# Transposes of weighted values and of the last state as pairs of 64-row tiles over two banks, with the step orders written anew

## The chip, the cores and the metric

The kernel runs on one core of one Trainium2 chip. The metric is the device time of one execution in microseconds (us). Each kernel is timed several times, and the median is compared.

## The reference, cut to what matters

The input `x` is 64 batches of 64 rows by 256 columns, and `ctx` has the same shape. Four cross-attention layers follow one another:

```python
# layer 0: attention over the 256 columns of each batch, with 64x64 weights
Mn = Wn @ inorm(x) + bn;  Mm = Wm @ inorm(ctx) + bm
A  = softmax(Mn^T Mm);    x = Wo @ (Wl @ ctx + bl) A^T + bo + x
# layers 1 and 2: 16 heads of 16 over the 64 rows of a batch
a = layer_norm(ctx, gamma, beta)
Q = x @ Wq.T;  K = a @ Wk.T;  V = a @ Wv.T
out = softmax(Q K^T / 4) V                 # per batch and head
x = x + tanh(gate) * (out @ Wo.T)
# layer 3: one head over 256 columns, keys and values from ctx
x = x + alpha * (softmax((x @ Wq.T)(ctx @ Wk.T)^T / 16) (ctx @ Wv.T)) @ Wo.T
```

Everything is float32. The products that need the precision are made of three passes over split operands (a `_hi` part and a `_lo` part).

## The kernel before, in words

The 64 batches are worked on in 8 groups of 8. A group is 512 tokens, and the state lies in SBUF with features on the partitions and tokens along the free axis. A prologue loads and prepares the weights and does layer 0 of the first group. Each pass of the loop then does layers 1, 2 and 3 of its group, and beside them layer 0 and the layer norm of the next group. The last pass has no next group.

The order of work on TensorE (PE), ScalarE (ACT) and VectorE (DVE) is written out by hand in tables (lines 38 to 66), one for each engine, with a second set for the prologue. A word such as `T2.0-1` is a step of a layer and its indices. Each engine runs its own table in strict order, and semaphores tie the three together. The steps that are spoken of below:

- `xT`, `cT`: transposes of the next group's x and ctx (L453), copied out by ACT (L776, L780). `nT`: the normalised ctx (L468). `Mn`, `Mm`: the two products of layer 0 (L525).
- `V1`, `V2`, `V3`, `K1`, `K2`, `K3`, `Q1`, `Q2`: projections (L389 to L391). ACT copies V out at L807, K at L795, Q at L818.
- `S1`, `S2`: scores of layers 1 and 2 in eight strips (L656). DVE takes the maximum (L1055) and writes the shifted scores (L1059), of which there are two buffers. ACT takes the exponential (`X`, L856).
- `T1`, `T2`: transposes of the probabilities (L677) and ACT's copies (L870). `A1`, `A2`: probabilities times values (L731). DVE normalises them into `attn` (L1098, L1100).
- `AT1`, `AT2`: transposes of half a group's `attn` (L544). ACT copies the result to `attnT_hi` (L822), then DVE writes the rest as `attnT_lo` (L1022).
- `O1`, `O2`: output projections of both parts (L389 to L391). DVE adds them to the state (L1031). `H` and `L` split the state (ACT L837, DVE L990) for the next `Q`.
- `S0`, `X0`, `T0`, `A0`: layer 0 of the next group (L641, L851, L677/L872, L724).
- `S3`, `X3`, `T3`, `PV`: layer 3. `XN`: the state after layer 2, transposed back to tokens by features (L552, ACT copy L826), to which DVE adds `PV` (L1043).

Every step that fills PSUM takes the next of the 8 banks in the order of PE's table (`fills_of`, L108). So a fill waits until the eighth fill before it has been read. A step may take one or two banks; `turn_halves` (L671) transposes each 128-row block as two 64-row halves, the upper into one bank and the lower into another.

Of the kernel before, what the change touches and what calls it, by code (L numbers as in the profile page):

```python
# [21 lines left out]
P = 128  # L22
# [37 lines left out]
    cT.0 xT.0-1 cT.1 Wq1.0 Wk1.0 NM.1 NM.0 TG.0 Wo1.0 Wq2.0 Wv1.0 Wk2.0 Mn.0-1 Mm.0-1 Wo3T.0 nT.0-1 KB.1 VW3.0 X0.0-2 M3.0  # L60
    X0.3 T0.0-1 X0.4 T0.2-3 X0.5 Wv2.0 X0.6-7 T0.4 VB1.0 T0.5 Wo2.0 KB.2 T0.6-7 H.0 K1.0 VB2.0 OB.1 Q1.0 K1.1 H.1 OB.2
# [1289 lines left out]
```

## Time and profile before

| | us |
|---|---|
| median of 3 runs | 617.71 (616.09 to 618.76) |
| the profiled execution | 619.04 |
| its span, first to last instruction | 616.9 |
| PE busy | 570.0 |
| DVE busy | 469.0 |
| ACT busy | 469.4 |
| POOL busy | 118.0 |

The busy times are sums over the whole span. The loop repeats every 70.3 us, so a steady pass is best read as four stretches, named here by the steps at their ends. All examples are from the pass that begins at 269.5 us. Matmuls overlap one another, so what a step costs PE is the time from its first instruction to that of the next step, and not the sum of the durations.

### The profile page before, as it was taken

Reading aid. Unit: us, or ns where it says so; the run is one execution under the profiler, and the core shown is the slowest. Engines: PE = TensorE matmul, PEld = TensorE weight load, DVE = VectorE, ACT = ScalarE, POOL = GpSimd, SP = SyncE. Lnnn points to the kernel's source line nnn. Section 1 sums busy time; section 2 is a strip of 40 time slices with the busy share of each in tenths; the row PEclk is TensorE's granted clock in tenths of the full one; section 3 lists DMA queues with packets and bytes.
Section 4 is the critical chain, followed back from the end, with each engine's and each line's share of the span. In section 5 each row is a group of like instructions: output and inputs, shape, how many; then the busy total and the mean of one; then the engine's idle time right before and its main releaser. Section 6 shows DMA issues by size and latency. Waiting matters only on the chain.

```text
span 616.9 us, 25805 instructions
## 1 busy us (share of the span) xinstructions
PE 570.0 (92%) x10867; PEld 502.2 (81%) x10867; DVE 469.0 (76%) x1023; ACT 469.4 (76%) x961; POOL 118.0 (19%) x132
## 2 busy tenths in 40 slices
PE   1799999999999999999999999999999999999885
PEld 1678788888888887988889887998889888998774
DVE  5785879676986879687786869778796869876553
ACT  0799878878787779867788869867788768868651
POOL 3503070103310070102500060101601051000000
PEclk9899999999999999999999999999999999999978
DMA  6420001110020100210020100210020100010001
GB/s 154 161 75 2 2 3 44 35 37 1 3 75 4 34 2 4 74 36 2 2 75 3 36 2 3 74 36 3 2 75 2 37 2 2 3 36 3 3 2 34
DMA packets 18499, 18.32 MB, mean 30 GB/s; under 512 B 1828, under 2 KB 18340, under 8 KB 18404
## 3 DMA queue, kind: packets, MB, share of 16 engines
q1 hardware_dynamic: 18024, 16.55, 8.5%
q8 instruction: 87, 1.43, 1.0%
q0 software_dynamic: 320, 0.26, 0.4%
q14 instruction: 8, 0.07, 0.0%
q10 hardware_dynamic: 60, 0.01, 0.0%
HBM read 12.63 MB, written 4.19 MB: 27 GB/s over the span
## 4 chain that ended last, share of the span: by engine, by line
PE 65%; DVE 15%; ACT 10%; issue 6%; DMA 1%; SPq 1%; POOL 0%; DVEq 0%; ACTq 0%; POOLq 0%
PE psum L389 10%; PE psum L731 8%; PE psum L677 8%; PE psum L391 8%; PE psum L390 8%; DVE negmax L1055 7%; PE psum L724 5%; DVE shifted L1059 4%; PE psum L641 4%; ACT work L856 3%; PE psum L656 3%; PE psum L544 3%; ACT v L807 2%; PE psum L453 2%; DMA mrow_u<-in_mask_dram 1%
## 5 line engine op out<-in xcount | busy, mean ns | idle before, releaser
L1059 DVE TENSOR_TENSOR shifted<-psum,negmax 128x512 f32<-128x512 f32 x128 | 88.5, 692 | 10.5 <-ACT work L856 5.6
L856 ACT ACTIVATE work<-shifted 128x512 f32<-128x512 f32 x128 | 79.1, 631 | 18.8 <-DVE shifted L1059 17.8
L870 ACT ACTIVATE work<-psum,group_mask 128x512 f32<-128x512 f32 x128 | 80.4, 696 | 16.4 <-PE psum L677 16.4
L1055 DVE TENSOR_REDUCE negmax<-psum 128x8 f32<-128x512 f32 x128 | 87.3, 682 | 5.9 <-PE psum L656 5.3
L677 PEld LDWEIGHTS psum<-const,work 64*128 64x128 f32 x1536 | 55.8, 141 | 33.4 <-issue 32.0
L677 PE MATMUL psum<-const,work 64*128 64x64 f32 x1536 | 65.0, 229 | 18.7 <-ACT work L856 16.6
L731 PEld LDWEIGHTS psum<-v,work 128*64 128x64 f32 x2048 | 63.9, 141 | 8.1 <-issue 5.9
L731 PE MATMUL psum<-v,work 128*64 128x34 f32 x2048 | 67.5, 227 | 0.0
L851 ACT ACTIVATE work<-psum,negmax 128x256 f32<-128x256 f32 x128 | 50.2, 511 | 12.2 <-DVE negmax L1051 12.2
L807 ACT ACTIVATE v<-psum 64x256 f32<-64x256 f32 x128 | 49.7, 388 | 10.0 <-PE psum L391 8.7
L795 ACT ACTIVATE kbd<-psum,own_bias,const 128x512 f32<-128x512 f32 x64 | 46.2, 777 | 4.8 <-PE psum L391 4.4
L1051 DVE TENSOR_REDUCE negmax<-psum 128x2 f32<-128x512 f32 x64 | 40.5, 682 | 9.2 <-PE psum L641 9.2
L1244 POOL TENSOR_SCALAR var_eps<-mean_var 128x8 f32<-128x8 f32 x8 | 2.0, 248 | 221.4 <-DVE mean_var L1116 221.4
L1022 DVE TENSOR_TENSOR attnT_lo<-psum,attnT_hi 128x512 fp32r<-128x512 f32 x32 | 22.1, 689 | 26.0 <-ACT attnT_hi L822 26.0
L389 PE MATMUL psum<-attnT_hi,wT_o_hi 128*128 128x256 f32 x128 | 39.4, 308 | 1.7 <-DVE attnT_lo L1022 0.3
L656 PE MATMUL psum<-kbd,work 32*64 32x128 f32 x2048 | 39.3, 283 | 1.2 <-ACT kbd L795 0.9
L389 PE MATMUL psum<-wT_v_hi,nT_hi 128*128 128x256 f32 x128 | 39.3, 307 | 0.0
L872 ACT ACTIVATE work<-psum 128x512 f32<-128x512 f32 x64 | 35.6, 616 | 4.6 <-PE psum L677 4.6
L724 PE MATMUL psum<-v,work 128*64 128x65 f32 x1024 | 36.7, 223 | 0.5 <-issue 0.5
L390 PE MATMUL psum<-attnT_lo,wT_o_hi 128*128 128x256 f32 x128 | 36.7, 287 | 0.0
L391 PE MATMUL psum<-attnT_hi,wT_o_lo 128*128 128x256 f32 x128 | 36.6, 286 | 0.0
L389 PE MATMUL psum<-state_hi,wT_q_hi 128*128 128x256 f32 x128 | 36.5, 285 | 0.0
(181 smaller groups left out, 1536.1 us busy)
## 6 DMA issues: line engine op xcount, KB each, us to landing
x_raw<-in_x_dram SPq DMA_DIRECT2D x8, 512.0 KB, 4.3
c_raw<-in_ctx_dram SPq DMA_DIRECT2D x8, 512.0 KB, 5.0
...
```

The source lines that it names most:

```text
L389: pe.matmul(o, lh, rh, start=first, stop=False)
L390: pe.matmul(o, lh, rl, start=False, stop=False)
L391: return pe.matmul(o, ll, rh, start=False, stop=last)
L656: mm_ = pe.matmul(to[C * c:C * c + C, P * n:P * n + P], queries[rows, k, C * b:C * b + C], kbd[l - 1][rows, k, b].rearrange("p q s -> p (q ...
L677: mm_ = pe.transpose(banks[h][:, C * n:C * n + C], src[rows], ident[rows, rows])
L724: mm_ = pe.matmul(o[C * q:C * q + C, cols], probsT[:, at + q, t0:t0 + C], v0[:, batch_of(i), s, :], start=s == 0, stop=s == 1)
L731: mm_ = pe.matmul(o[C * c:C * c + C, 2 * VW * j:2 * VW * (j + 1)], probsT[:, at + c, C * j:C * j + C], v2[l - 1][:, 2 * i + c, j].rearrang ...
L807: ins = act.activation(values[C * q:C * q + C, c, q, :, :, 0:HD], o[C * c:C * c + C, :].rearrange("k (p j q v) -> k q p j v", p=2, q=2, v= ...
L856: act.activation(probs[:, exp_row(g, l, i, last), :], shifted[:, i % 2, :], ACT.Exp).then_inc(exps, 1)
L870: act.activation(probsT[:, at, :], o[:], ACT.Copy, scale=group_mask[:, 2 * i + c:2 * i + c + 1]).then_inc(free, 1)
L1055: dve.tensor_reduce(negmax[:, i % 2, :], sv, AX_X, ALU.max, negate=True).then_inc(rowmax, 1)
L1059: dve.tensor_tensor(shifted[:, i % 2, :].rearrange("t (j k) -> t j k", k=C), sv, negmax[:, i % 2, :].unsqueeze(2).broadcast_to([P, NJ, C]) ...
```

## The change

`AT` was four transposes of 128 by 128 into one bank. It is now `turn_halves`: eight transposes of 64 rows by 128 columns, four into each of two banks. ACT and DVE copy each bank by itself, half the tokens of every pair at a time, so each has two instructions of 128x256 where it had one of 128x512. `XN` was two steps of four transposes; it is now one step of sixteen over two banks, and still two copies of 128x512 on ACT.

```diff
@@ fills_of
-            if kind == "P" or kind == "S" or kind == "A" and (l or i % 2 == 0):
+            if kind == "P" and l in ("AT1", "AT2"):
+                fills += [step + (c,) for c in range(2)]
+            elif kind == "P" or kind == "S" or kind == "A" and (l or i % 2 == 0):
@@ TensorE, proj_step
                 elif name in ("AT1", "AT2"):
-                    for q in range(2):
-                        for k in range(NK):
-                            mm_ = pe.transpose(o[:, (2 * q + k) * P:(2 * q + k + 1) * P],
-                                               attn[:, 2 * i + q, NJ * k:NJ * k + NJ, :].rearrange("t n d -> t (n d)"), ident)
+                    o2, signal2 = start_fill(g, step, last, 1)
+                    turn_halves((o, o2), (signal, signal2), [attn[:, 2 * i + q, NJ * k:NJ * k + NJ, :].rearrange("t n d -> t (n d)")
+                                                             for q in range(2) for k in range(NK)])
+                    return
...
                 elif name == "XN":
-                    for q in range(2):
-                        p = 2 * i + q
-                        for k in range(NK):
-                            mm_ = pe.transpose(o[:, D * q + P * k:D * q + P * k + P], state[:, k, P * p:P * p + P], ident)
+                    o2, signal2 = start_fill(g, ("P", "XN", 1), last)
+                    turn_halves((o, o2), (signal, signal2), [state[:, k, P * p:P * p + P] for p in range(NP) for k in range(NK)])
+                    return
@@ ScalarE, proj_step
                 elif name in ("AT1", "AT2"):
-                    o, _ = filled(g, step, last)
-                    act.activation(attnT[0][:].rearrange("f k (p t) -> f p k t", p=2),
-                                   o[:].rearrange("f (p k t) -> f p k t", p=2, k=NK), ACT.Copy).then_inc(attn_hi, 1)
+                    for h in range(2):
+                        o, _ = filled(g, step, last, h)
+                        act.activation(attnT[0][:].rearrange("f k (p h t) -> f h p k t", p=2, h=2)[:, h],
+                                       o[:, 0:4 * C].rearrange("f (p k t) -> f p k t", p=2, k=NK), ACT.Copy).then_inc(attn_hi, 1)
@@ VectorE, proj_step
                 elif name in ("AT1", "AT2"):
...
+                    for h in range(2):
+                        o, free, _ = filled(g, step, last, h)
+                        dve.wait_ge(attn_hi, 8 * g + (4 * int(name[2]) - 3 + 2 * i + h))
+                        hi, lo = [t[:].rearrange("f k (p h t) -> f h p k t", p=2, h=2)[:, h] for t in attnT]
+                        dve.tensor_tensor(lo, o[:, 0:4 * C].rearrange("f (p k t) -> f p k t", p=2, k=NK), hi.bitcast(F32),
+                                          ALU.subtract).then_inc(free, 1)
```

All six tables are written anew. A line of PE's, for example:

```diff
-    V1.0 S1.0-3 V2.0 Q1.1 V3.0 S1.4-7 T1.0-1 V1.1 K3.0 A1.0-1 T1.2-3 xT.0-1 AT1.0 K2.0 O1.0 A1.2-3 K2.1 AT1.1 Q2.0 O1.1
+    V1.0 S1.0-3 Q1.1 V2.0 V3.0 S1.4-7 T1.0-1 K3.0 V1.1 A1.0-1 T1.2-3 AT1.0 K2.0 O1.0 A1.2-3 K2.1 AT1.1 Q2.0 O1.1 S2.0-3
```

Three places matter. The first is on PE in the middle of layer 1, from `A1.0-1` to the start of `K2.0`. Before:

```order
L731 MATMUL psum<-v_1,work 64x34 x32
L677 MATMUL psum<-const,work 128x64 x32
L453 MATMUL psum<-const,x_raw 128x64 x16
L544 MATMUL psum<-const,attn 128x128 x4
L389 MATMUL psum<-nT_hi,wT_k_hi 128x512
L390 MATMUL psum<-nT_lo,wT_k_hi 128x512
```

And after (line numbers are those of the changed kernel, L678 is `turn_halves`):

```order
L732 MATMUL psum<-v_1,work 64x34 x32
L678 MATMUL psum<-const,work 128x64 x32
L678 MATMUL psum<-const,attn 128x64 x8
L391 MATMUL psum<-nT_hi,wT_k_hi 128x512
L392 MATMUL psum<-nT_lo,wT_k_hi 128x512
```

The transposes of x (`xT`) have left this place, and the four transposes of `attn` are eight of half the columns.

The second place is on ACT around the first strips of layer 2's scores. `state_hi` is `H.3`, `shifted` the exponentials `X2`, `v_2` is `V2.1`, `scratch` is `V3.1`, and the `work<-psum` of 128x2x256 is `Q2.1`. Before:

```order
L837 ACTIVATE state_hi<-state 128x512
L856 ACTIVATE work<-shifted 128x512
L807 ACTIVATE v_2<-psum 64x2x8x16 x4
L856 ACTIVATE work<-shifted 128x512
L769 REGISTER_ALU
L815 ACTIVATE scratch<-psum 128x512
L818 ACTIVATE work<-psum 128x2x256
L856 ACTIVATE work<-shifted 128x512 x2
L789 ACTIVATE mn_hi<-psum,scale_col 128x512 x2
```

And after:

```order
L840 ACTIVATE state_hi<-state 128x512
L770 REGISTER_ALU
L777 ACTIVATE xT<-psum 128x8x64
L859 ACTIVATE work<-shifted 128x512
L858 REGISTER_ALU
L859 ACTIVATE work<-shifted 128x512
L770 REGISTER_ALU
L808 ACTIVATE v_2<-psum 64x2x8x16 x4
L777 ACTIVATE xT<-psum 128x8x64
L816 ACTIVATE scratch<-psum 128x512
L858 REGISTER_ALU
L859 ACTIVATE work<-shifted 128x512
```

Both copies of `xT` now stand here, and the second exponential comes ahead of `V2.1`. On DVE the split of the state, `L.3`, has moved in the same place from behind the first strip to behind the second.

The third place is on PE towards the end of a pass, from `S3.1` on. Before:

```order
L667 MATMUL psum<-scratch,state 64x64 x8
L724 MATMUL psum<-v,work 64x65 x24
L552 MATMUL psum<-const,state 128x128 x4
L701 MATMUL psum<-const,probs 128x128
L389 MATMUL psum<-nT_hi,wT_k_hi 128x512
```

And after:

```order
L668 MATMUL psum<-scratch,state 64x64 x8
L678 MATMUL psum<-const,work 128x64 x16
L678 MATMUL psum<-const,state 128x64 x16
L702 MATMUL psum<-const,probs 128x128
L391 MATMUL psum<-state_hi,wT_q_hi 128x256
```

`XN` is one step ahead of `T3.0`, `Q1.0` comes before `K1.1`, and the last of layer 0's `A0` steps (L724) now follow `T3.1`, directly ahead of `PV`. On ACT the copies of `T3.1`, `XN`, `Q1.0` and `K1.1` and the split `H.1` follow one another in that order at the end of the pass, and on DVE `L.1` stands behind `PV`.

## Rows read from the trace of the kernel before

**Rows 1.** The page's part 4: chain that ended last, share of the span by engine.
```profile
PE 65%; DVE 15%; ACT 10%; issue 6%; DMA 1%; SPq 1%; POOL 0%; DVEq 0%; ACTq 0%; POOLq 0%
```

**Rows 2.** Busy time by window: start:end, length, PE, PEld, DVE, ACT, POOL, clock.
```profile
277.30:297.40 20.10, 19.85 (x346) 17.54 (x346) 13.86 (x38) 14.76 (x28) 8.07 (x8) 1.00 0.01 2
297.40:311.75 14.35, 13.66 (x305) 11.50 (x299) 13.94 (x22) 12.37 (x24) 3.50 (x3) 1.00 0.01 2
311.75:339.80 28.05, 27.93 (x542) 25.18 (x542) 21.28 (x52) 22.60 (x49) 2.76 (x5) 1.00 0.14 43
269.50:277.30 7.80, 6.80 (x165) 6.21 (x164) 7.29 (x13) 6.38 (x14) 0.00 (x0) 1.00 0.21 69
```

**Rows 3.** Timeline, 284.6 to 287.6: start us, duration us, engine, line, tiles, count.
```profile
284.71 0.72 PE L453 MATMUL psum<-const,x_raw 64*128 64x64 f32 x16
...
285.36 0.66 PE L544 MATMUL psum<-const,attn 128*128 128x128 f32 x4
...
285.77 0.48 PE L389 MATMUL psum<-nT_hi,wT_k_hi 128*128 128x512 f32 x1
...
286.06 0.60 ACT L822 ACTIVATE attnT_hi<-psum 128x512 fp32r<-128x512 f32 x1 [1.49 <-PE psum L544]
...
286.69 0.69 DVE L1022 TENSOR_TENSOR attnT_lo<-psum,attnT_hi 128x512 fp32r<-128x512 f32 x1 [0.71 <-ACT attnT_hi L822]
...
287.52 0.35 PE L389 MATMUL psum<-attnT_hi,wT_o_hi 128*128 128x256 f32 x1
```

**Rows 4.** Timeline of PE, 322 to 329: `T0.0-3`, then `XN.0` and `O2.1`.
```profile
322.58 1.22 PE L677 MATMUL psum<-const,work 64*128 64x64 f32 x32
323.60 0.36 PE L641 MATMUL psum<-mm_hi,mn_hi 64*128 64x256 f32 x2
...
328.44 0.66 PE L552 MATMUL psum<-const,state 128*128 128x128 f32 x4
328.85 0.36 PE L389 MATMUL psum<-attnT_hi,wT_o_hi 128*128 128x256 f32 x1
```

**Rows 5.** Lines, shapes apart: count, busy us, mean ns of one, idle before.
```profile
L1100 DVE TENSOR_TENSOR attn<-psum,recip 128x256 f32<-128x256 f32 x64 | 27.2, 424 | 2.2
...
L544 PE MATMUL psum<-const,attn 128*128 128x128 f32 x128 | 20.9, 288 | 0.0
...
L776 ACT ACTIVATE xT<-psum 128x512 f32<-128x512 f32 x16 | 8.6, 586 | 0.3 <-PE psum L453 0.3
```

**Rows 6.** Timeline of ACT in the prologue: a copy of 128x256 from PSUM.
```profile
53.15 0.40 ACT L883 ACTIVATE scratch<-psum 128x256 f32<-128x256 f32 x1
```

**Rows 7.** Timeline, 297 to 312: `H.3`, `X2.0`, `V2.1`, `Mn`, `S2.4`, `cT`.
```profile
297.31 0.63 ACT L837 ACTIVATE state_hi<-state 128x512 fp32r<-128x512 f32 x1 [1.66 <-DVE state L1031]
...
298.89 0.63 ACT L856 ACTIVATE work<-shifted 128x512 f32<-128x512 f32 x1 [0.94 <-DVE shifted L1059]
...
299.43 1.57 ACT L807 ACTIVATE v<-psum 64x256 f32<-64x256 f32 x4
...
304.12 1.25 ACT L789 ACTIVATE mn_hi<-psum,scale_col 128x512 fp32r<-128x512 f32 x2
...
304.82 1.41 DVE L1016 SCALAR_TENSOR_TENSOR mn_lo<-psum,scale_col,mn_hi 128x512 fp32r<-128x512 f32 x2
...
306.24 0.69 DVE L1055 TENSOR_REDUCE negmax<-psum 128x8 f32<-128x512 f32 x1
...
311.77 0.43 PE L453 MATMUL psum<-const,c_raw 64*128 64x64 f32 x7
```

**Rows 8.** Timeline, end of a pass: `H.1` on ACT, the next pass's `S1.0-3`.
```profile
337.96 0.62 ACT L837 ACTIVATE state_hi<-state_in 128x512 fp32r<-128x512 f32 x1
...
339.81 1.21 PE L656 MATMUL psum<-kbd,work 32*64 32x128 f32 x64
```

**Rows 9.** Busy time by window, the end of the prologue and the first steps.
```profile
45.00:77.00 32.00, 29.20 (x488) 25.49 (x488) 22.27 (x55) 28.70 (x69) 5.69 (x7) 1.00 0.01 2
```

**Rows 10.** Busy time by window in the last pass; the clock is third from last.
```profile
595.00:605.00 10.00, 9.84 (x112) 8.88 (x110) 2.93 (x7) 3.43 (x6) 0.00 (x0) 0.50 0.01 2
```

More of the change, by code:

```diff
@@ L38 @@
 PE_ORDER = """
-    V1.0 S1.0-3 V2.0 Q1.1 V3.0 S1.4-7 T1.0-1 V1.1 K3.0 A1.0-1 T1.2-3 xT.0-1 AT1.0 K2.0 O1.0 A1.2-3 K2.1 AT1.1 Q2.0 O1.1
-    S2.0-3 V2.1 V3.1 Q2.1 V0.0-1 Mn.0-1 T2.0 S2.4-7 T2.1 K3.1 Mm.0-1 A2.0-1 cT.0-1 T2.2 nT.0-1 AT2.0 T2.3 S0.0-3 A2.2-3
-    O2.0 AT2.1 K1.0 T0.0-3 S0.4-7 A0.0-1 S3.0 A0.2-3 T0.4-5 XN.0 O2.1 T3.0 T0.6-7 A0.4 S3.1 A0.5-7 XN.1 T3.1 K1.1 Q1.0
+    V1.0 S1.0-3 Q1.1 V2.0 V3.0 S1.4-7 T1.0-1 K3.0 V1.1 A1.0-1 T1.2-3 AT1.0 K2.0 O1.0 A1.2-3 K2.1 AT1.1 Q2.0 O1.1 S2.0-3
+    xT.0-1 V2.1 V3.1 Q2.1 V0.0-1 Mn.0-1 T2.0 S2.4-7 T2.1 Mm.0-1 K3.1 A2.0-1 cT.0-1 T2.2 nT.0-1 T2.3 A2.2 AT2.0 S0.0-3 A2.3
+    O2.0 T0.0-1 AT2.1 K1.0 T0.2-3 S0.4-7 A0.0-2 S3.0 A0.3 T0.4-5 O2.1 A0.4-5 S3.1 T0.6-7 XN.0-1 T3.0 Q1.0 K1.1 T3.1 A0.6-7
     PV.0-1
@@ L44 @@
 ACT_ORDER = """
-    SC.0 V1.0 X1.0 V2.0 Q1.1 X1.1-2 V3.0 X1.3 T1.0 X1.4-5 T1.1 X1.6 K3.0 X1.7 V1.1 AT1.0 T1.2-3 H.2 xT.0-1 K2.0 AT1.1 K2.1
-    Q2.0 H.3 X2.0 V2.1 X2.1 V3.1 Q2.1 X2.2-3 Mn.0-1 T2.0-1 X2.4 K3.1 X2.5 Mm.0 X2.6 Mm.1 X2.7 cT.0-1 T2.2 nT.0-1 AT2.0
-    T2.3 X0.0-3 AT2.1 K1.0 T0.0-3 X0.4-7 T0.4 X3.0 H.0 T0.5-7 XN.0 T3.0 X3.1 T3.1 XN.1 K1.1 Q1.0 H.1
+    SC.0 V1.0 Q1.1 X1.0-1 V2.0 X1.2 V3.0 X1.3 T1.0 X1.4 T1.1 X1.5 K3.0 X1.6-7 V1.1 AT1.0 T1.2-3 H.2 K2.0 AT1.1 K2.1 Q2.0
+    H.3 xT.0 X2.0-1 V2.1 xT.1 V3.1 X2.2 Q2.1 X2.3 Mn.0-1 T2.0-1 Mm.0 X2.4-5 K3.1 Mm.1 X2.6-7 cT.0-1 T2.2 nT.0-1 T2.3 AT2.0
@@ L48 @@
+    X0.0-3 AT2.1 T0.0-1 K1.0 T0.2-3 X0.4-6 T0.4-5 X0.7 X3.0 H.0 X3.1 T0.6 T3.0 T0.7 T3.1 XN.0-1 Q1.0 K1.1 H.1
 """
 DVE_ORDER = """
-    S1.0-7 A1.0 ST.0 A1.1 ST.1-2 AT1.0 ST.3 MV.0 O1.0 A1.2-3 L.2 AT1.1 O1.1 S2.0 L.3 S2.1-3 V0.0-1 Mn.0-1 S2.4-7 Mm.0-1
-    A2.0-1 cT.0-1 nT.0-1 AT2.0 S0.0-1 A2.2-3 S0.2-3 O2.0 AT2.1 S0.4-7 S3.0 A0.1 A0.3 O2.1 S3.1 A0.5 X3.0 L.0 X3.1 A0.7 L.1
-    PV.0-1
+    S1.0-7 ST.0 A1.0-1 ST.1 AT1.0 ST.2-3 O1.0 MV.0 A1.2 L.2 A1.3 AT1.1 O1.1 S2.0-1 L.3 S2.2-3 V0.0-1 Mn.0-1 S2.4-7 Mm.0-1
@@ L53 @@
+    A2.0-1 cT.0-1 nT.0-1 A2.2 S0.0 AT2.0 S0.1-2 A2.3 S0.3 O2.0 AT2.1 S0.4-6 A0.1 S3.0 S0.7 A0.3 O2.1 L.0 A0.5 X3.0 S3.1
+    X3.1 A0.7 PV.0-1 L.1
 """
 PE_FIRST = """
-    MT.0 W0T.0 GT.0 MS.0 cT.0-1 xT.0-1 W0.0 Wq1.0 Wk1.0 Wo1.0 Wq2.0 V0.0-1 Wv1.0 Wk2.0 Mn.0-1 Mm.0-1 Wo3T.0 nT.0-1 VW3.0
-    S0.0-3 M3.0 T0.0-1 S0.4-5 T0.2-3 S0.6-7 A0.0 Wv2.0 A0.1-3 T0.4-5 Wo2.0 VB1.0 T0.6-7 A0.4 K1.0 A0.5 K1.1 VB2.0 A0.6-7
-    Q1.0
+    MT.0 MS.0 GT.0 xT.0-1 cT.0-1 Wq1.0 W0T.0 Wk1.0 Wv1.0 nT.0-1 Mn.0-1 Mm.0-1 W0.0 Wo3T.0 S0.0-3 V0.0-1 Wq2.0 M3.0 Wk2.0
@@ L58 @@
+    VB1.0 T0.0-3 S0.4-5 Wo1.0 VW3.0 S0.6-7 A0.0-1 T0.4-5 Wv2.0 A0.2 K1.0 A0.3 T0.6-7 VB2.0 Wo2.0 A0.4-5 K1.1 A0.6-7 Q1.0
 """
 ACT_FIRST = """
[L60 to L61 removed]
+    xT.0-1 cT.0-1 Wq1.0 NM.1 NM.0 Wk1.0 Wv1.0 Mn.0-1 Mm.0 nT.0-1 Mm.1 Wo3T.0 KB.1 X0.0 TG.0 X0.1 Wq2.0 X0.2-3 M3.0 Wk2.0
@@ L62 @@
+    T0.0 VB1.0 T0.1-3 X0.4 Wo1.0 X0.5 VW3.0 KB.2 X0.6-7 T0.4 Wv2.0 T0.5 Wo2.0 T0.6-7 H.0 K1.0 OB.1 VB2.0 K1.1 Q1.0 H.1
+    OB.2
 """
 DVE_FIRST = """
-    MT.0 WB.0 ON.0 MS.0 ST.0 W0T.0 GT.0 ST.1-2 TG.0 ST.3 MV.0 NB.0 Wq1.0 cT.0-1 W0.0 Wk1.0 Wo1.0 Wq2.0 Wv1.0 V0.0-1 Wk2.0
-    Mn.0-1 Mm.0-1 nT.0 S0.0 nT.1 S0.1-2 VW3.0 S0.3 M3.0 S0.4-7 Wv2.0 A0.1 A0.3 Wo2.0 L.0 A0.5 A0.7 L.1
+    MT.0 MS.0 GT.0 WB.0 TG.0 ST.0-3 MV.0 cT.0 NB.0 W0T.0 cT.1 Wq1.0 ON.0 Wk1.0 Mn.0 Wv1.0 Mn.1 nT.0-1 Mm.0-1 W0.0 S0.0-3
@@ L66 @@
+    V0.0-1 Wq2.0 M3.0 Wk2.0 S0.4-6 Wo1.0 VW3.0 A0.1 S0.7 Wv2.0 A0.3 Wo2.0 L.0 A0.5 A0.7 L.1
 """
@@ L488, in proj_step @@
                     return
-                if name == "PV" and i:
+                if name in ("PV", "XN") and i:
                     return
-                used = {"O1": [("P", "AT1", i)], "O2": [("P", "AT2", i)], "PV": [("T", 3, 0), ("T", 3, 1)]}.get(name, [])
+                used = {"O1": [("P", "AT1", i, h) for h in range(2)], "O2": [("P", "AT2", i, h) for h in range(2)], "PV": [("T", 3, 0), ("T", 3, 1)]}.get(name, [])
                 if name in ("AT1", "AT2"):
@@ L820, in proj_step @@
                 elif name in ("AT1", "AT2"):
-                    o, _ = filled(g, step, last)
-                    act.activation(attnT[0][:].rearrange("f k (p t) -> f p k t", p=2),
-                                   o[:].rearrange("f (p k t) -> f p k t", p=2, k=NK), ACT.Copy).then_inc(attn_hi, 1)
+                    for h in range(2):
+                        o, _ = filled(g, step, last, h)
+                        act.activation(attnT[0][:].rearrange("f k (p h t) -> f h p k t", p=2, h=2)[:, h],
+                                       o[:, 0:4 * C].rearrange("f (p k t) -> f p k t", p=2, k=NK), ACT.Copy).then_inc(attn_hi, 1)
                 elif name == "XN":
                     o, free = filled(g, step, last)
-                    act.activation(result[:, 2 * i:2 * i + 2, :], o[:].rearrange("s (q h) -> s q h", q=2), ACT.Copy).then_inc(free, 1)
+                    act.activation(result[:].rearrange("t p (k h f) -> t h p k f", k=NK, h=2)[:, i],
+                                   o[:].rearrange("t (p k f) -> t p k f", p=NP, k=NK), ACT.Copy).then_inc(free, 1)
             def state_high(g, n, last):
@@ L979, in _, with filled @@
         def _(dve):
-            def filled(g, step, last):
-                bk, n = fill(g, step, last)
+            def filled(g, step, last, c=0):
+                bk, n = fill(g, step, last, c)
                 dve.wait_ge(full[bk], n)
```

6 lines of the change are left out of this document (removed).

## The prediction

> **What bounds the kernel now.** I read the chain of waits first, then the busy time by window over one steady pass, then the timeline inside each window. The chain is PE for 65% of the span, DVE for 15% and ACT for 10% [rows 1], so neither "PE is the bound" nor its opposite holds everywhere. The windows show where each is true [rows 2]. A pass takes 70.3 us and falls into four stretches:
>
> - A, from `T1.0` to `S2.0-3`, 20.1 us: PE busy 19.85. PE sets the pace.
> - B, from the first strips of `S2` to `cT`, 14.35 us: DVE busy 13.94, PE 13.66. DVE sets the pace with ACT close beside it.
> - C, from `cT` to the next pass's `S1.0-3`, 28.05 us: PE busy 27.93. PE sets the pace.
> - D, from `S1.0-3` to `T1.0`, 7.8 us: PE busy 6.80. `T1.0` waits for the exponentials of four strips, that is for DVE and ACT.
>
> So PE time removed in A and C is worth itself. The same time removed in B or D is worth nothing, and work added there to ACT or DVE costs.
>
> **The transposes on PE.** Four transposes of 128x128 hold PE from 285.36 to 285.77, 0.41 us [rows 3]. The new form is not unknown: `turn_halves` is already used for the probabilities, where 32 pieces of 64 columns take 1.02 us, 32 ns each [rows 4]. Eight pieces are 0.26 us, so an `AT` saves 0.15 us. The mean duration of one transpose, 288 ns, is latency and doesn't enter [rows 5]. `XN` before is two steps of about 0.41 [rows 4]; sixteen pieces are 0.51; saved 0.31.
>
> **The chain behind AT.** In A, `AT1` is followed by one projection and then by `O1`, which needs both parts of the result. From the transposes to `O1` it takes 2.16 us: 0.70 to ACT's start, 0.63 to DVE's start, 0.83 to `O1` [rows 3]. PE's own work in between is 0.41 plus about 1.48 for six matmuls of 512 columns, so some 0.27 is stall, twice a pass. After the change: 0.70 less 0.15 is 0.55; ACT's first copy of 128x256 takes 0.40 [rows 6] and DVE starts 0.43 after it; DVE's two of 0.424 each [rows 5] run while ACT's second is done, 0.85; then the same 0.14 to PE. Together 1.97, saved 0.2 for each of `AT1.0` and `AT1.1`. The bounds are 0 (ACT or DVE is late with other work) and 0.4 (the whole stall and the 0.15 go). `AT2.0` and `AT2.1` in C have other steps behind them and give the 0.15 each.
>
> Two copies instead of one make ACT longer by 2 x 0.40 - 0.60 = 0.2 and DVE by 2 x 0.42 - 0.69 = 0.16 per `AT`, 0.8 and 0.64 us per pass. In A and C they are covered: ACT is busy 14.76 of 20.10 and 22.60 of 28.05 [rows 2]. The register instructions that the table adds on ACT are bounded by the same cover.
>
> **The move of xT.** It leaves A, where its sixteen transposes hold PE from 284.71 to 285.36, 0.65 us [rows 3]: all of it gained. `AT1.0` comes nearer to `A1.1`, but `T1.2-3` still stands between. SP's loads wait for `nT`, which isn't moved against its neighbours, and none is near.
>
> It goes to B, where PE has 0.7 us of slack but ACT has two more copies of 0.586 [rows 5]. `xT.0` fits into the 0.94 us in which ACT waits for the first shifted strip [rows 7]. The second doesn't, and here the new order matters more: `X2.1` now stands ahead of `V2.1`. The second strip comes one DVE pace (0.68 + 0.69 less overlap, 1.32 us) after the first, so not before 298.89 + 1.32 = 300.21. Before, ACT began `V2.1` at 299.43 and reached `Mn` at 304.12, 4.7 us later, with about 0.35 idle [rows 7]. Now it has the same instructions, less that idle, plus `xT.1` at about 0.5: 300.21 + 4.85 = 305.05, late by 0.9. DVE's `Mn` (304.82) needs ACT's, and the strips `S2.4-7` (306.24) come behind it, then `cT` at 311.77 [rows 7]. I take +0.8 for B. Bounds: 0 if DVE has slack that I don't see, +1.2 if both copies count in full.
>
> **The rest of the orders.** In C, saved 2 x 0.15 + 0.31 = 0.6. `T0.2-3` is held apart from `T0.0-1` and `A0.2` comes early, which may cost a few tenths behind ACT. In D, `Q1.1` goes ahead of `X1.0` on ACT; ACT's sum is unchanged, but it must wait for PE's `Q1.1`: +0.2 (0 to 0.5). At the end of the pass `L.1` stands behind `PV` on DVE and `H.1` behind four copies on ACT. Before, `H.1` ended at 338.58, 1.2 us ahead of `S1.0-3` at 339.81 [rows 8]. I charge nothing in the sum, and a rival below has the rest.
>
> **The sum.** Per pass: A -0.65 - 2 x 0.2 = -1.05; B +0.8; C -0.6; D +0.2; together -0.65 us. Seven passes have a next group: -4.6. The last has no `xT` and no front, so A gives -0.4 and C -0.6, part of it at the lower clock: for 595 to 605 the granted clock is 0.50, which is 1.2 GHz [rows 10], and every PE price there doubles, +0.2 more. Last pass -1.2. The prologue's statistics and first products come earlier, but ACT must do the same work before `S1.0-3` and is already busy 28.70 of 32.00 at its end [rows 9]: 0, bounds -1.5 and +1.5. In all -5.8 us on the profiled execution's 619.04 (span 616.9 and 2.1 around it), 613.2. That execution is 1.3 above the median of the runs shown, so against the median 617.71 - 5.8 = 611.9, rounded to 612.
>
> **The rivals.**
>
> 1. B costs nothing and the whole chain gain in A comes. For it: ACT idles 2 us of B's 14.35. Against: `Mn` sits right behind the dense part. Then each pass gives 0.65 + 0.8 + A's 0.55 + C's 0.6 less D's 0.2, less what I doubt, about 1.5 us: 7 x 1.5 + 1.2 = 12, 606.
>
> 2. The gain is given back and nothing is left. PE's 1.65 us per pass in A and C meet +1.2 in B, +0.5 in D: 7 x 0 to 1, some 1.2 from the last pass: 616.5. For it: ACT and DVE each get some 0.7 us more per pass, and B and D, 22 of 70 us, are theirs. A page speaks for this side: the Trainium skill, "TensorEngine Tiling (Array Packing)", section "PSUM Bottleneck", says that tiling speeds up TensorE but not the copies out of PSUM, which may then be the bottleneck. By that rule alone the sum would stand at this rival's figure. The trace agrees for B and D and disagrees for A and C.
>
> 3. Slower: the end of the pass becomes a queue. ACT gets to `K1.1` only after `T3.1`, two copies of `XN` at some 0.5 and `Q1.0` at 0.5; PE behind `T3.1` has `A0.6-7`, `PV` and `V1.0`, about 3.6 us, before `S1.0-3` needs `K1.1`. ACT needs 0.3 + 1.0 + 0.5 + 1.45 = 3.3, then `H.1` 0.6, and DVE's `L.1` 0.7 and the first strip behind it. It decides from 0.4 us of lateness of `T3.1`'s partner copies on. If `S1` strips start 1.3 us late, D grows by that, and with B at +1.2 a pass loses 0.9: 7 x 0.9 - 1.2 = +5, 623. Against it: the `A0` and `K1.1` steps give ACT slack earlier.
>
> 4. The change doesn't do what it says: the row pairs of `attn` run one behind another. Then 8 pieces cost no less than 4, A and C lose 0.9 per pass against the forecast: 618. Against it: the same form runs at 32 ns a piece now [rows 4], from the same kind of source.
>
> **How the numbers follow.** The forecast has 0.43, with its own range 609 to 614.5; rival 1 has 0.21, rival 2 0.20, rival 3 0.12, rival 4 0.04. A difference under 0.5%, 3.1 us, can't be told from no change. Faster by more: the forecast and rival 1, 0.64, and a share of rival 2, 0.03: 0.67. Same: the rest of rival 2, rival 4 and a bit of 3: 0.22. Slower: 0.11. The range 605.5 to 619 holds rival 1 and 2 and leaves out rival 3 and the far end of rival 1.
>
> **What would show it.** Right: the steady pass falls from 70.3 to about 69.6; from `AT1.0` to `O1.0` it takes about 1.95 us; eight pieces of `attn` hold PE 0.26; ACT starts `Mn` some 7.6 us after `H.3` and not 6.8; B is longer than 14.35 by 0.6 to 1; C is shorter by about 0.6. Wrong: B unchanged (rival 1), D above 8.5 with `S1.0-3` waiting for ACT's K copy (rival 3), or 64-column pieces of `attn` over 50 ns apart (rival 4). A lower clock in a steady pass would upset all of it; there it is 1.00 now [rows 2].

## The result, and the profile after

The changed kernel is slower: 625.73 us, median of 6 runs, beside 618.5 for the kernel before; ratio 1.0124, 95% interval 1.0106 to 1.0142. The forecast was 612, in a range of 605.5 to 619, with 0.11 for slower. It was wrong in size and in sign.

The profiled span went from 616.9 to 624.4 us. The chain is still PE's, more than before [rows 1]:

```profile
PE 69%; ACT 13%; DVE 8%; issue 7%; DMA 2%; SPq 1%; DVEq 0%; ACTq 0%
```

The same four stretches, in the order A, B, C, D of [rows 2] (columns as there):

```profile
281.60:299.53 17.93, 17.78 (x274) 15.91 (x275) 12.49 (x38) 13.83 (x27) 4.95 (x5) 1.00 0.01 2
299.53:315.77 16.24, 15.68 (x379) 13.25 (x379) 14.96 (x24) 13.45 (x26) 7.15 (x6) 1.00 0.01 3
315.77:344.35 28.58, 27.91 (x559) 24.77 (x559) 22.31 (x56) 22.79 (x52) 2.77 (x5) 1.00 0.15 41
273.58:281.60 8.02, 6.74 (x164) 6.20 (x164) 6.90 (x12) 6.10 (x14) 0.00 (x0) 1.00 0.22 69
```

These windows end at the first strips of `S2` (299.53). [rows 2] put that edge at 297.40, which is a little inside `S2`; with the edge at the first strip in both kernels (296.30 before) and D's end at `T1.0` (277.34, 281.64), a pass compares so, in us:

| stretch | before | after | change | forecast |
|---|---|---|---|---|
| D | 7.80 | 8.06 | +0.26 | +0.2 |
| A | 18.96 | 17.89 | -1.07 | -1.05 |
| B | 15.47 | 16.24 | +0.77 | +0.8 |
| C | 28.04 | 28.58 | +0.54 | -0.6 |
| pass | 70.27 | 70.77 | +0.50 | -0.65 |

Three terms of four came as priced. C has the wrong sign. Two more things lie outside the table: the first `S1.0-3` starts at 60.99 instead of 57.19 us (the prologue, forecast 0), and the last pass takes 66.45 instead of 66.53 (forecast -1.2). The seven passes together take 496.96 instead of 493.18, 3.78 more. With 3.80 for the prologue and -0.08 for the last pass, that is the whole 7.5 us of the span.

The chain behind `AT1.0` in A, as in [rows 3], is 1.89 us from the pieces to `O1.0` (forecast 1.97; before 2.16):

```profile
289.14 0.46 PE L678 MATMUL psum<-const,attn 64*128 64x64 f32 x8
...
289.61 0.66 ACT L824 ACTIVATE attnT_hi<-psum 128x256 fp32r<-128x256 f32 x2 [0.71 <-PE psum L678]
...
290.02 0.76 DVE L1027 TENSOR_TENSOR attnT_lo<-psum,attnT_hi 128x256 fp32r<-128x256 f32 x2 [0.70 <-ACT attnT_hi L824]
...
291.03 0.28 PE L391 MATMUL psum<-attnT_hi,wT_o_hi 128*128 128x256 f32 x1
```

The eight pieces hold PE 0.39 here, not 0.26. What the four `AT` steps cost, from the first transpose to the next step's first instruction, is this:

| step | before | after |
|---|---|---|
| `AT1.0` | 0.41 | 0.39 |
| `AT1.1` | 0.36 | 0.40 |
| `AT2.0` | 0.58 | 0.28 |
| `AT2.1` | 0.35 | 0.35 |

Here are the lines of `AT2.1`, before and then after, each with the first instruction of `K1.0` behind it:

```profile
320.66 0.60 PE L544 MATMUL psum<-const,attn 128*128 128x128 f32 x4
321.01 0.48 PE L389 MATMUL psum<-nT_hi,wT_k_hi 128*128 128x512 f32 x1
```

```profile
325.14 0.41 PE L678 MATMUL psum<-const,attn 64*128 64x64 f32 x8
325.49 0.50 PE L391 MATMUL psum<-nT_hi,wT_k_hi 128*128 128x512 f32 x1
```

A piece is still 32 ns behind the last. But where PE changes between 64-row pieces and full-array matmuls, about 0.1 us is added: sixteen pieces of `T0` hold PE 0.64 ahead of a full-array step (331.69 to 332.33) and 0.55 ahead of other pieces (335.65 to 336.20). `AT2.0` now stands between two tiled steps and gains; the others have a full-array step behind them. `XN` is 0.59 (336.20 to 336.79), where its two steps were 0.41 and 0.50.

At the end of the pass, to be compared with [rows 8], the three engines do this:

```profile
341.03 1.09 PE L559 MATMUL psum<-scratch 64*64 64x256 f32 x16
...
341.66 1.47 ACT L796 ACTIVATE kbd<-psum,own_bias,const 128x512 f32<-128x512 f32 x2
...
342.44 1.66 DVE L1046 SCALAR_TENSOR_TENSOR attn<-psum,recip,attn 128x256 f32<-128x256 f32 x4 [0.18 <-issue]
...
344.35 0.62 PE L657 MATMUL psum<-kbd,work 32*64 32x128 f32 x25 [0.60 <-DVE attn L1046]
```

`V1.0` begins at 342.05 and, with the 1.62 us that it took before, would be through at 343.67. `S1.0-3` starts 0.68 later, when DVE has read `PV`. The waits (line, releaser, total us, times, longest) say that it is so in every pass:

```profile
PE psum L657 <- DVE attn L1046: 4.3, 7, 0.6
PE psum L678 <- issue: 0.8, 2, 0.6
```

The reason is in the bank numbers, which follow the order of fills and begin again at 0 in every pass. Before, PE's order has 104 fills, thirteen rounds of 8. Four `AT` with two banks make 108, so at the pass boundary the fills of banks 0 to 3 no longer look back 8 fills but 4: `PV.0` and `PV.1` take banks 2 and 3, and `S1.1` and `S1.2`, four fills later, take the same ones. (The fills of banks 4 to 7 look back 12.)

In the prologue (windows of before, then of after), `nT` and the next steps stand earlier and PE runs into two waits. The first is 2.99 us ahead of `nT` at 23.84. The profile names no releaser, but ACT's last copy of the normalised ctx ends at 23.63. The second is 2.81 us ahead of `S0.0-3` at 33.72, for DVE. Behind each, PE's pieces take about double, and from 32 to 40 us the granted clock is near its lower level. The kernel before has one such place, 2.32 us idle ahead of 23.79 and a clock of 0.63 behind it:

```profile
24.00:28.00 4.00, 3.62 (x75) 3.29 (x74) 2.04 (x7) 3.97 (x10) 2.13 (x2) 0.63 0.01 4
...
32.00:36.00 4.00, 3.60 (x59) 2.96 (x50) 3.35 (x6) 3.94 (x15) 0.00 (x0) 1.00 0.26 79
36.00:40.00 4.00, 3.62 (x44) 2.96 (x42) 3.67 (x8) 3.67 (x11) 0.00 (x0) 1.00 0.60 206
```

```profile
24.00:28.00 4.00, 3.97 (x84) 3.08 (x87) 0.99 (x3) 3.16 (x9) 1.17 (x1) 1.00 0.02 4
...
32.00:36.00 4.00, 2.28 (x21) 2.31 (x23) 2.49 (x7) 2.87 (x12) 0.00 (x0) 0.61 0.00 0
36.00:40.00 4.00, 4.00 (x77) 3.59 (x75) 3.23 (x6) 2.12 (x6) 0.00 (x0) 0.53 0.11 9
```

### The profile page after: what moved, and what is told of

Its sections match the earlier page's. It is cut to its first block, busy times and chain, and to the rows that moved or that the text cites. A ratio compares the mean times of both kernels' runs of the same rounds, so it can differ in the third digit from the quotient of the medians.

```text
span 624.4 us, 26526 instructions
## 1 busy us (share of the span) xinstructions
PE 571.1 (91%) x11059; PEld 501.8 (80%) x11059; DVE 471.5 (76%) x1055; ACT 469.9 (75%) x993; POOL 121.9 (20%) x132
## 4 chain that ended last, share of the span: by engine, by line
PE 69%; ACT 13%; DVE 8%; issue 7%; DMA 2%; SPq 1%; DVEq 0%; ACTq 0%
PE psum L678 12%; PE psum L391 10%; PE psum L732 10%; PE psum L393 8%; PE psum L392 8%; PE psum L725 5%; ACT work L859 4%; PE psum L657 4%; PE psum L642 4%; ACT v L808 3%; DVE negmax L1058 3%; DVE shifted L1062 2%; DVE attn L1046 2%; PE psum L470 2%; PE psum L668 1%
## 5 line engine op out<-in xcount | busy, mean ns | idle before, releaser
L678 PE MATMUL psum<-const,work 64*128 64x64 f32 x1536 | 65.4, 229 | 18.2 <-ACT work L859 17.5
L678 PEld LDWEIGHTS psum<-const,work 64*128 64x128 f32 x1536 | 55.5, 140 | 31.3 <-issue 28.6
L732 PE MATMUL psum<-v,work 128*64 128x34 f32 x2048 | 69.3, 227 | 0.9 <-ACT work L873 0.9
L854 ACT ACTIVATE work<-psum,negmax 128x256 f32<-128x256 f32 x128 | 51.9, 507 | 11.1 <-DVE negmax L1054 11.1
L1054 DVE TENSOR_REDUCE negmax<-psum 128x2 f32<-128x512 f32 x64 | 41.8, 684 | 16.6 <-PE psum L642 16.2
L391 PE MATMUL psum<-state_hi,wT_q_hi 128*128 128x256 f32 x128 | 38.6, 302 | 0.6 <-DVE state_lo L993 0.5
L657 PEld LDWEIGHTS psum<-kbd,work 32*64 32x64 f32 x2048 | 31.8, 133 | 8.7 <-issue 5.8
L1027 DVE TENSOR_TENSOR attnT_lo<-psum,attnT_hi 128x256 fp32r<-128x256 f32 x64 | 24.1, 419 | 18.9 <-ACT attnT_hi L824 18.9
L391 PE MATMUL psum<-wT_v_hi,nT_hi 128*128 128x256 f32 x128 | 37.6, 294 | 0.0
L824 ACT ACTIVATE attnT_hi<-psum 128x256 fp32r<-128x256 f32 x64 | 21.4, 395 | 21.2 <-PE psum L678 21.2
```

The source lines that it names most:

```text
L391: pe.matmul(o, lh, rh, start=first, stop=False)
L657: mm_ = pe.matmul(to[C * c:C * c + C, P * n:P * n + P], queries[rows, k, C * b:C * b + C], kbd[l - 1][rows, k, b].rearrange("p q s -> p (q ...
L678: mm_ = pe.transpose(banks[h][:, C * n:C * n + C], src[rows], ident[rows, rows])
L732: mm_ = pe.matmul(o[C * c:C * c + C, 2 * VW * j:2 * VW * (j + 1)], probsT[:, at + c, C * j:C * j + C], v2[l - 1][:, 2 * i + c, j].rearrang ...
L854: ins = act.activation(probs[:, exp_row(g, 0, i, last), D * u:D * u + D], psum[bk][:, D * u:D * u + D], ACT.Exp, bias=negmax0[:, i, u:u + 1])
```

## The experiments

Ratios are to the kernel before, timed beside each kernel. "A quiet pass" is the one that begins near 270 us; it takes 70.27 before and 70.77 after.

### The prologue's order alone

```diff
 changed kernel, with the kernel before's PE_FIRST, ACT_FIRST, DVE_FIRST
```

> The changed kernel with the three prologue tables of the kernel before; the loop is the changed one. Theory: the first S1.0-3 comes 3.8 us later in the changed kernel (60.99 against 57.19) because of the prologue's new order, so this kernel should be 3.8 us faster than the changed one, about 622, with S1.0-3 first at about 57.2. Rival: the prologue's delay comes from outside the tables (loads, memsets); then it stays at 625.7.

Measured: 1.0072 (1.0049 to 1.0095), first `S1.0-3` at 57.64, quiet pass 70.80, `S1.0-3` still waits for DVE 4.3 us. The theory held: 0.5 of the 1.24% is the prologue, about 3 us, give or take the 0.2 of each interval.

### TensorE kept busy in the prologue

```diff
-                    for k in range(NK):
+                    for _ in range(8 if name == "Wv1" else 1):   # and the loops under it, one deeper
```

> The changed kernel, with the four transposes of Wv1's first tile written eight times over into the same bank (same values), so that TensorE works in the prologue where it stood idle ahead of 23.84 us. Theory (after the idle TensorE runs at half its clock and its pieces take double, and this makes the prologue late): pieces of that stretch near 1.2 instead of 2.0 us, the first S1.0-3 1 to 3 us earlier, 622.5 to 624.5. Rival (the order, three more loads of weights ahead of T0.0, sets it): no change, 625.

Measured: 1.0126 (1.0084 to 1.0168), no gain in time. In the trace the first `S1.0-3` is at 59.84, 1.15 earlier. Two lines of PE:

```profile
24.03 1.16 PE L470 MATMUL psum<-mix,c_norm 64*64 64x64 f32 x64
...
26.93 1.07 PE L527 MATMUL psum<-c_norm,w0T 64*64 64x256 f32 x16
```

They were 1.98 and 1.96 in the changed kernel. So the doubled pieces do come from the idle time ahead of them, but what follows waits for DVE anyway (2.71 us before `S0.0-3`), the clock falls there (0.50 in 32 to 36), and most is lost again. Theory and rival each hold for a part. In another run of the same prologue (the run of moved banks, below) the clock was 1.00 from 32 us on and `S1.0-3` came at 58.29. From these single executions the order costs about 1 us, and the later fall of the clock adds up to 2.7 where it happens.

### The transposes alone, and the ring of banks

Three kernels ask what the second bank costs. The first is the kernel before with only `AT` changed; the second adds skipped banks to it so that the boundary closes; the third has no change but the skipped banks.

```diff
 kernel before; AT1 and AT2 as in the changed kernel, XN and all tables as before
```

> The kernel before with AT1 and AT2 alone as pairs of 64-row tiles over two banks; XN, all six tables as before. Theory: AT1.0 and AT1.1 to O1 fall from 2.1 to 1.9 us, AT2 gives 0.1 each, about 0.6 us less per pass, but 108 fills break the ring: S1.0-3 waits for DVE's PV, which ends at 340.87 in the pass where S1.0-3 starts at 339.81, so a pass gains about 1.1 - 0.6 = 0.5: some 618 + 3.5 = 621.5. Rival (the form is a gain wherever it stands): 614.

```diff
 the same, one bank skipped ahead of each of V1.1, K2.0, T0.4, A0.4
```

> As the run before with the ring closed by four skipped banks. Theory: 0.6 us less per pass and nothing given back, 8 passes: 618 - 5 = 613.5. Rival (ACT's and DVE's second instruction per AT cost what PE saves): 618.

```diff
 kernel before, AT as it was; one bank skipped ahead of each of K2.0, Q2.0, T2.3, K1.0
```

> The kernel before with its transposes of 128x128 in one bank as they were; only one bank of the ring is skipped behind each of the four AT steps (before K2.0, Q2.0, T2.3, K1.0), so that the fills behind find the same banks as with two-bank transposes. Theory (the second bank is the price that the two-bank transposes alone paid, 636): 632 to 637. Rival (the 64-row form itself costs, not its bank): within 1% of the kernel before, 618 to 622.

Measured: 1.0295 (1.0238 to 1.0352), 1.0612 (1.0554 to 1.0671) and 1.039 (1.0336 to 1.0444). Waits of the first and of the third:

```profile
PE psum L391 <- ACT work L873: 9.1, 7, 1.3
PE psum L658 <- DVE attn L1046: 8.9, 7, 1.4
...
PE psum L679 <- DVE cT_lo L1009: 4.0, 7, 0.6
```

```profile
PE psum L664 <- DVE attn L1051: 9.1, 7, 1.4
PE psum L397 <- ACT work L878: 8.8, 7, 1.3
...
PE psum L685 <- DVE cT_lo L1014: 3.5, 7, 0.5
```

The same three waits, though the third kernel has not one 64-row transpose more. The price is the bank, not the form: a step with two banks brings the fills behind it one nearer to the step whose bank they need. `K2.0` behind `AT1.0` then needs `T1.2`'s bank, which ACT hasn't read. I had expected the direction of the first but a fifth of its size. The second I had wrong: skipping more banks closes the boundary and shortens the distance elsewhere. The third is dearer than the 632 to 637 I gave it (641.36), and dearer than the first, so the form gives a little back; no run separates that part.

So in the old order this transpose loses 18 us, and the changed kernel loses 7. Counted by its table, `K2.0` there takes a bank of `A1.0`, because `xT`'s two fills no longer stand in between. No run takes the other orders and `XN` apart from this.

```diff
 changed kernel, one bank skipped ahead of each of K3.0, K2.0, T0.4, T0.6
```

> The changed kernel with banks skipped at four loose places, so that the 108 fills of a pass take 112 places, a whole number of rounds of 8. Theory: 108 is 4 over a multiple of 8 and each pass starts again at bank 0, so S1.1 and S1.2 of a pass get the banks of PV.0 and PV.1, filled just before, and S1.0-3 waits for DVE's PV; closing the ring takes off 0.65 us in each of 7 passes, 4.5 us: about 621, the step V1.0 to S1.0 back at 1.6 us from 2.3. Rival: S1.0-3 waits for ACT's K1.1 copy (343.13) or Q1.0 anyway, or the skipped banks make as much wait elsewhere: 625.

Measured: 1.0191 (1.0138 to 1.0243), quiet pass 70.99. The wait of `S1.0-3` for DVE is gone and others stand in its place: PE's projections now wait 4.5 us for DVE's shifted scores, 15 times. The rival was right.

### Moving only the boundary's banks

```diff
+    MOVED = {("P", "PV", 0, 0): 5, ("P", "PV", 1, 0): 4, ("S", 1, 3, 0): 6, ("P", "V2", 0, 0): 4}
+            banks.update({f: b for f, b in MOVED.items() if f in banks})
```

> The changed kernel, except that four fills at the end of a pass take other banks (PV.0 bank 5, PV.1 bank 4, S1.3 bank 6, V2.0 bank 4), so that the scores S1.0-3 need no bank that PV.0 or PV.1 used. Theory (the pass boundary's banks are the price of stretch C): the 4.3 us that TensorE waits for VectorE's attn at S1.0-3 are gone, seven times about 0.65 us: about 621. Rival (another wait takes its place, ScalarE's K1.1 or Q1.0 end as late as PV's copy): within 0.5% of the changed kernel, 625.

> As the run before, and with the prologue's three order tables of the kernel before. Theory (prologue and pass boundary are the two causes of the loss and add up): about 617 to 618, level with the kernel before. Rival (only the prologue counts): 622, as with the old prologue alone.

Measured: 1.0175 (1.0132 to 1.0218, four runs) and 1.009 (1.0062 to 1.0119), where the kernels without the moved banks had 1.0124 and 1.0072. No gain in time, and the rival of each was right. Quiet passes are 70.56 and 70.60, only 0.2 less. The trace of the first names the new wait, for `XN`'s copies:

```profile
337.80 1.08 ACT L835 ACTIVATE attn<-psum 128x512 f32<-128x512 f32 x2
...
339.03 1.09 PE L566 MATMUL psum<-scratch 64*64 64x256 f32 x16 [0.35 <-ACT attn L835]
```

ACT had stood idle 0.95 us ahead of these copies, for `T3.1`, which its order puts first.

```diff
-    ... T0.7 T3.1 XN.0-1 Q1.0 ...
+    ... T0.7 XN.0-1 T3.1 Q1.0 ...
```

> The changed kernel with the kernel before's prologue tables, the four moved banks at the end of the pass, and on ScalarE the two copies of XN ahead of T3.1's scratch copy instead of behind it (ScalarE idled 0.92 us there before T3.1 while XN lay ready, and TensorE's PV then waited 0.35 us for XN's banks). Theory (the pass boundary's wait had only moved to XN's copies): the PV wait goes, S1.0-3 starts 0.35 us earlier in each pass, ratio to the kernel before 1.004 to 1.006 against 1.009 without this edit. Rival (another wait behind it, K1.1 or the strips, takes it again): 1.009.

Measured: 1.0041 (1.0017 to 1.0065), quiet pass 70.19. `PV` starts when `A0.6-7` is through:

```profile
334.18 1.10 ACT L836 ACTIVATE attn<-psum 128x512 f32<-128x512 f32 x2
...
336.20 1.09 PE L567 MATMUL psum<-scratch 64*64 64x256 f32 x16
```

The theory held. The moved banks had given 0.2 us a pass and the copy order gives 0.4 behind them, 0.58 together. In the ratio the copy order is 0.5% (from 1.009), both together 0.3% (from the 1.0072 of the old prologue alone), with intervals of 0.2 to 0.3; seven times 0.58 would be 0.66%. The copy order without the moved banks wasn't run.

### The orders in D and B

```diff
-PE    V1.0 S1.0-3 Q1.1 V2.0 V3.0          ACT   V1.0 Q1.1 X1.0-1 V2.0 X1.2 V3.0
+PE    V1.0 S1.0-3 V2.0 Q1.1 V3.0          ACT   V1.0 X1.0 V2.0 Q1.1 X1.1-2 V3.0
```

> As the run before, and with Q1.1 behind X1.0 and V2.0 again on ScalarE and TensorE, as in the kernel before. Theory (Q1.1 ahead of X1.0 is what made stretch D 0.26 us longer): D back at 7.8 us, 7 x 0.26 = 1.8 us less, ratio 1.002. Rival (D is longer because PE's 64-row order and ST moved): D unchanged, same time.

```diff
-ACT   xT.0 X2.0-1 V2.1 xT.1 V3.1 X2.2
+ACT   xT.0 X2.0 V2.1 xT.1 X2.1 V3.1 X2.2
```

> As the run before, and on ScalarE X2.1 again behind V2.1 instead of ahead of it. Theory (X2.1 ahead of V2.1 makes ScalarE wait for the second strip and V2.1, V3.1, Mn late; that is half of stretch B's 0.77): S2.0 to S2.4 9.56 falls to 9.2, 2 to 2.5 us less, ratio 0.998 to 1.0. Rival (xT's two copies alone set B): B unchanged at 9.56.

> The best kernel so far once more, in five rounds. Theory (0.5 us less a pass than the kernel before, less two stalls of about 1 us together): ratio 0.996 to 0.998, faster by 1 to 2 us. Rival (level): 0.999 to 1.001.

Both kernels also move `Q1.1` to bank 5, where the changed kernel has it.

Measured: 1.0004 (0.9983 to 1.0025), 0.9988 (0.9959 to 1.0016), and the last again in five rounds 0.9987 (0.997 to 1.0004). Quiet passes 69.80, 69.70, 69.80. D's order was worth what I had given it and a little more (0.39 us a pass, of which D itself is 0.37). B's shows its own sign: from `S2.0` to `S2.4` it takes 9.15 instead of 9.56. But 0.29 of that is lost again ahead of `cT`, so a pass gains only 0.1. The third run met its rival, level (0.999 to 1.001), and not the 0.996 to 0.998 of its theory. The final kernel's stretches, as D, A, B, C:

```profile
267.58:275.35 7.77, 6.77 (x166) 6.25 (x166) 7.31 (x13) 6.38 (x14) 0.00 (x0) 1.00 0.21 70
275.35:293.24 17.89, 17.80 (x274) 15.89 (x275) 12.75 (x38) 13.82 (x27) 4.97 (x5) 1.00 0.01 2
293.24:309.36 16.12, 15.66 (x380) 13.24 (x379) 14.83 (x24) 13.55 (x26) 7.13 (x6) 1.00 0.01 3
309.36:337.28 27.92, 27.85 (x559) 24.75 (x559) 21.51 (x54) 22.48 (x51) 2.76 (x5) 1.00 0.15 43
```

69.70 in all, 0.57 less than before: close to the 0.65 forecast, but with other parts. C is 0.12 shorter, not 0.6. No kernel here beats the kernel before by more than the comparison can tell.

### XN alone, its place alone, and idle time that nothing explains

```diff
 kernel before; XN as in the changed kernel, at XN.1's place; ACT: T3.0 X3.1 XN.0-1 T3.1
```

> The kernel before with only XN changed: one step of sixteen 64-row transposes over its two banks, placed where XN.1 stood, and ScalarE's two copies ahead of T3.1. Attn's transposes, xT, every other place and the count of fills as in the kernel before. Theory (the form pays where it takes no more banks): XN 0.41 + 0.50 becomes 0.59, 0.3 us less a pass, 616.4 less 2.2: 614 to 615 where the kernel before has 616.4, ratio 0.9965. Rival (XN's late place brings T3.1, K1.1 and S1.0-3 late): ratio 1.002 or more.

```diff
 kernel before; XN's full transposes kept, only moved to that place
```

> The kernel before with XN's two steps of full transposes as they were, but both at the late place (XN.0 beside XN.1, and ScalarE's two copies ahead of T3.1) where the run with XN alone in row pairs had them. Theory (the added instructions of the row pairs bring stalls in which TensorE waits for nothing in the trace, not the place): ratio 0.998 to 1.002, passes of 70.3 without such stalls. Rival (the late place delays T3.1, K1.1 and S1.0-3): 1.005 to 1.008, as with the row pairs.

Measured: 1.0069 (1.0041 to 1.0097) and 1.0067 (1.0051 to 1.0083), as both rivals had it. The place costs, and the form then gives or takes nothing that can be told. My theory that the added instructions bring the loss fell. Where the second kernel loses its 4 us isn't shown: its profiled execution is its fastest (615.8), and there the quiet pass is only 0.14 longer than before. The first kernel's trace shows the step at 0.65 instead of 0.91 in a quiet pass, and in other passes this:

```profile
335.13 0.34 PE L676 MATMUL psum<-const,state 64*128 64x64 f32 x4
...
335.89 0.59 PE L676 MATMUL psum<-const,state 64*128 64x64 f32 x12 [0.42 <-issue]
```

PE stops in the middle of a step, waiting for nothing that the profile shows. The kernel before has such stops too: 0.49 us inside `A0` at 115.99, and one inside `S0` in its pass of 70.7, which only the weight loads show:

```profile
246.17 0.18 PEld L641 LDWEIGHTS psum<-mm_hi,mn_lo 64*128 64x128 f32 x1 [0.34 <-issue]
```

To see whether it hangs on where the code lies, two kernels got the same 28 extra matmuls in the prologue:

```diff
 kernel before, and the kernel of 0.9988: Wv1's four transposes eight times over
```

> The kernel before, with the four transposes of Wv1's first tile written eight times over into the same bank in the prologue, 28 matmuls more there and the same code in the passes. Theory (where blocks of instructions begin decides which passes stall): the prologue 0 to 3 us later, and some passes 0.4 to 1.1 us longer than 70.2, with idle time of TensorE that nothing in the trace explains. Rival (the kernel before has instructions to spare): every pass within 0.2 us of 70.3 and only the prologue changed.

> The best kernel so far (changed transposes, the kernel before's prologue order, moved banks, XN's copies ahead of T3.1, the old orders in D and B), with the same 28 matmuls more in the prologue. Theory (position of the code): the passes that take 70.6 us there now fall on other passes, and their sum changes by 1 us or more in either direction. Rival (the stall belongs to the late passes, whatever the code's place): passes 1 to 4 at 69.7, the last two at 69.9 and 70.6 again.

Measured: 1.0075 (1.005 to 1.01) and 1.0061 (1.0045 to 1.0077). The first `S1.0-3` is at 60.90 and 61.04, 3.7 and 3.3 us later, which is most of it: the step became 3.3 us longer at a place where PE had no idle time, and it costs its full length. Passes of the first, from the second on, are 71.02, 70.97, 70.47, 70.51, 70.21, 70.24, against 70.2 to 70.7 before. The two long ones hold a stop of 0.68 and one of 0.50, as the theory had it and against the rival's 0.2 us around 70.3:

```profile
189.84 0.92 PE L725 MATMUL psum<-v,work 128*64 128x65 f32 x24 [0.68 <-issue]
```

Of the second, two passes (70.27 and 70.82) are long. But the kernel of 0.9988 had its long passes at different places in two executions of the same code (70.60 as the seventh; then 70.28, 70.32 and 70.42 as the second, fifth and seventh). So a stop that moves from one pass to another doesn't show that the code's place moved it, and the two runs settle nothing.

The page of the first `XN` kernel has an instruction queue with 88 packets and 1.44 MB, 16 KB each, 11 in each pass, as many as a pass of the kernel before has. The Trainium skill, "Runtime: NRT & Kernel Launch", section "Instruction fetch mechanics", says that instructions come in blocks of 16 KiB and that crossing from one to the next is mostly hidden. The trace agrees on the size; whether the idle time is a late block isn't shown by any run, and stays open. Its size can't be read from the waits put down to `issue`: between 120 and 560 us they are 1.9 and 2.7 us in the two runs of the best kernel, but most of that is a gap of 0.2 to 0.4 ahead of `T2`'s pieces, which other passes have too, put down to ACT or DVE.

## Why the prediction was wrong

**The bounds of the stretches.** Right: D, A and B came within 0.06 us of their terms.

**The transposes on PE.** The 32 ns a piece was right, the price of a step wasn't. "An `AT` saves 0.15 us" left out what PE pays where it changes between pieces and full-array matmuls. The four steps save 0.02, -0.04, 0.30 and 0.00: 0.28 in all instead of 0.60. That `AT2.0` and `AT2.1` together give the 2 x 0.15 of C is luck. `XN` saves 0.32 for 0.31 because the step before took 0.91, not twice 0.41. Rival 4 had the wrong mechanism, pieces one behind another, but what it said of the cost, eight pieces no less than four, came true at three steps of four.

**The chain behind AT.** Right, 1.89 for 1.97, and 1.88 behind `AT1.1` (2.11 before). What is gained is the stall ahead of `O1`, about 0.25 each time. ACT starts 0.47 behind the first piece instead of 0.70, while PE's own pieces save next to nothing there.

**xT.** Right in both halves, -0.65 in A and +0.77 in B. In B all of it comes ahead of `S2.4` (8.80 before, 9.57 after from `S2.0` on), and ACT starts `Mn` 7.53 us after `H.3`, as forecast (7.6). Of the reason given, `X2.1` ahead of `V2.1`, the run without it leaves 0.1 in B as a whole. That the two copies more on ACT are the rest is argued; no run took them out of B.

**"In C, saved 2 x 0.15 + 0.31 = 0.6".** This step failed. The saving is there, though not as priced (`AT2.0` 0.58 to 0.28, `AT2.1` 0.35 as before, `XN` 0.91 to 0.59), but two costs that I had put at nothing stand beside it. One is `S1.0-3`'s wait for `PV`'s banks, 0.68. I had looked for lateness at the end of the pass in ACT's queue (rival 3) and not in the banks, although the diff's first lines make two fills of one; counting them, 108 against a ring of 8, would have shown it. The other is 0.5 in small steps: the new order puts a tiled step where a full-array one stood behind `O2.0` and `O2.1`, and splits `A2.2-3`. `O2.1`, which was followed by a full transpose, took 1.51 from 328.85 [rows 4]. It is now followed by tiled `A0.4-5` and takes 1.62:

```profile
331.69 0.71 PE L678 MATMUL psum<-const,work 64*128 64x64 f32 x16
332.33 0.38 PE L391 MATMUL psum<-attnT_hi,wT_o_hi 128*128 128x256 f32 x1
...
333.95 0.45 PE L725 MATMUL psum<-v,work 128*64 128x65 f32 x8
```

Of the 0.11, 0.10 lies behind the twelve matmuls: `A0.4-5` starts 0.21 after the last of them (333.74), where the transpose had started 0.11 after it. `O2.0` went from 1.54 to 1.62, `A2` and `S3.1` lost 0.12 and 0.15. This part is read from the two traces, and no run took it away; in the best kernel it is still there.

**"I charge nothing" for the prologue.** This step failed too. The cover named was ACT's busy share of 45 to 77 [rows 9]. The loss comes before it, between 20 and 42 us, in a stretch that I hadn't read: PE idles twice, 2.99 and 2.81 us, and behind each idle time its pieces take double. It is 3.8 us in the trace and 0.5% in the ratio, outside my bound of +1.5.

**D.** The term was right, +0.26 for +0.2; undoing it gave 0.39 a pass.

**The last pass.** -1.2 was wrong; it is -0.1. Which of its steps take the gain back wasn't read.

**The miss in one line.** The forecast had -5.8 us of span and +7.5 came, 13.3 apart: C 8.0 (seven times 1.14), the prologue 3.8, the last pass 1.1, and 0.4 in passes longer than the one that the table shows.

**The rivals.** Rival 1's terms don't add up to its 1.5 us a pass: 0.65 and 0.8 are 1.45, and with the other two it is more than 2. B alone settles it, +0.77 and not 0. Rival 3 has the right sign, place and nearly the time (623), by another mechanism: DVE's `PV` and its banks, not ACT's `K1.1`. With 0.12 it was too small. Rival 2's cause, copies in B, took +0.77 as the forecast had it, and not the +1.2 that it needed. The Trainium skill, "TensorEngine Tiling (Array Packing)", section "PSUM Bottleneck", which the prediction put beside rival 2, says that copies out of PSUM may become the bottleneck. The trace agrees that they limit, at `S1.0-3`, but by when they free a bank rather than by their length.

The experiments take the loss away step by step, in per cent of the kernel before: prologue 0.5, end of the pass 0.3, D 0.4, B 0.2, from 1.24 down to -0.13. The steps between single kernels are about as large as their intervals; the total is not.
